# The next round's q1 and k projections put ahead of the probability transposes in a fused attention and mixture-of-experts layer

## The chip, the cores and the metric

One core of a Trainium2 chip runs the whole kernel. The metric is the device time of one execution in microseconds.

## The reference

The input x has 4 sequences of 512 tokens with 256 features. It is normalised over its features (xn). Two branches are computed from xn and multiplied:

```
xn  = layernorm(x)                                  # 2048 tokens x 256
q   = xn @ Wq   (16 heads x 128)      k, v = xn @ Wk, xn @ Wv   (4 key-value heads x 128)
q,k = rotary embedding with a per-position scale (q times it, k divided by it)
att = softmax(causal(q k^T / sqrt(128))) v          # four query heads share one key-value head
s   = att @ Wo
ffn = sum over the 2 best of 16 experts of weight * down(silu(gate) * up)  +  a shared expert
out = x + s * silu(ffn)
```

All of it is float32. The kernel keeps that precision on TensorE by splitting each operand into a float16 part ("hi") and a bfloat16 remainder ("lo") and adding three products, hi x hi, hi x lo and lo x hi (`PASSES`).

## The kernel before

Each engine has its own program, a queue worked off in the order in which it is written; semaphores tie the queues together. Nothing is planned at run time: the order on each engine is written out by hand in a function `round_` for each of them (POOL L605, ACT L781, DVE L1125, PE L1400).

Attention runs in 16 rounds, one for each pair of a sequence and a key-value head. A round has four query heads, and each head is a slot. Rounds 0 to 2 ("first", "second", "third") stand by themselves, as they also split weights and choose experts; rounds 3 to 14 are a hardware loop; round 15 is the last. While a round computes its attention, it also prepares the next round: the four query projections q0 to q3 and the key projection k of the next round are made in it, and the output projections o0 to o3 of the round before are finished in it. These share two PSUM banks, and an item waits until the item two before it has left its bank (`misc_free`).

What one head passes through, engine by engine:

- `score` (PE, L1341): q k^T of four query tiles in three units, one bank each, 12 matmuls. It waits for the lo halves of q and, in a round's first slot, of k (`rot_lo`, from POOL).
- `row_max` (DVE, L1057): mask and row maximum of each query tile, in the order of the units.
- `exponentials` (ACT, L733): exp and row sum of each tile.
- `invert_sums` (DVE, L1063): reciprocal of the four sums. It is called inside the rotation of a projection, behind that rotation's first product (L1039).
- `divide` (POOL, L533): the probabilities times those reciprocals. It releases `normed`.
- `transpose_probs` (PE, L1354): ten 128x128 transposes in three units over two banks. Units 0 and 1 (eight transposes) and unit 2 (two) are called apart. Unit 0 waits for `normed`; each unit waits for the bank that it shares with the second unit before it (`pt_lo`).
- `probs_hi` (ACT, L741) casts each unit out of PSUM, and `probs_lo` (DVE, L1069) subtracts that to get the remainder.
- `weigh_values` (PE, L1370), and `output_hi` (ACT, L756) and `output_lo` (DVE, L1075), which empty its bank.
- `project_out` (PE, L1386) and `add_projection` (DVE, L1082).

A projected q or k passes through `project` (PE, L1310, six matmuls of 512 columns), three products of the rotation (DVE, L1039, L1043, L1044), their sum (`rotate_sum`, POOL, L520), the cast to hi (`rotate_hi`, ACT, L721) and the subtraction for lo (`rotate_lo`, POOL, L527). In rounds 3 to 14 POOL also scatters the rows of one token tile to the experts, with two indirect DMAs (L550) behind slot 1's work; in round 1 and round 2 it computes the routing instead.

The order in slots 1 and 2 of a middle round, as each engine's `round_` has it (j is the slot, so head j is transposed while head j + 1 is scored):

- PE: score of head j + 1; transposes of units 0 and 1 of head j; projection (q1 in slot 1, k in slot 2); output projection j - 1; transposes of unit 2; weighing of head j - 1.
- ACT: output_hi of head 0 (slot 2 only); casts of units 0 and 1 of head j; exponentials of head j + 1; rotate_hi of q(j - 1); cast of unit 2.
- DVE: output_lo of head 0 (slot 2 only); row maxima of head j + 1; subtractions of units 0 and 1; the rotation of q1 or k, with the reciprocal of head j + 1 behind its first product; add_projection; subtraction of unit 2.
- POOL: sum of q(j - 1); divide of head j + 1; in slot 2 the sum of k; lo of q(j - 1); in slot 1 the scatter. Behind slot 2 come the lo of k, the sum of q2, the divide of the next round's head 0, and the lo of q2.

In slot 0 PE has score, projection q0, transposes of units 0 and 1, weighing of the round before's last head, values, transposes of unit 2; ACT and DVE there do the exponentials and the rotation ahead of the casts and subtractions. After slot 2 PE has projection q2, output projection o2, transposes of head 3 (units 0 and 1), weighing of head 2, the score of the next round's head 0, projection q3, transposes of unit 2, output projection o3.

Of the kernel before, what the change touches and what calls it, by code (L numbers as in the profile page):

```python
# [186 lines left out]
def build(nc, x, wq, wk, wv, wo, gate_t, w_gate_up, w_down, shared_gu, shared_down, rope, ident, mask, iota, tri, rows, digits, out):  # L187
    with ExitStack() as ctx:
# [1064 lines left out]
        def _(pe):  # L1253

            def transpose_xn(b, c, ps):
                for q in range(QT):
                    ins = pe.transpose(ps[:, q * P:(q + 1) * P], xn_t[:, b * QT + q, c * P:(c + 1) * P], ident_f[:])
                return ins

            def transpose_x_items(rd, items):  # L1260
                for name in items:
                    b, c = int(name[1]), int(name[2])
                    pe.wait_ge(xn_ready, b)
                    pe.wait_ge(misc_free, rd.item(name) - 2)
                    transpose_xn(b, c, misc_bank[rd.bank(name)]).then_inc(misc_ps, 1)
# [23 lines left out]
            def rank(rd):  # L1289
                pe.wait_ge(chosen, 1)  # L1290
                pe.wait_ge(zeroed, 2)
                pe.wait_ge(misc_free, rd.item("rank") - 2)
                ps, n = misc_bank[rd.bank("rank")], NT * E_ROUTED
                pe.matmul(ps[:, 0:n], tri_b[:], sel_b[:], start=True, stop=True)
                pe.matmul(ps[:, n:2 * n], ones_b[:], sel_b[:], start=True, stop=True).then_inc(misc_ps, 1)


            def project(rd, name):
                i, item, ps = rd.i + 1, rd.item(name), misc_bank[rd.bank(name)]
                b, g = i // NKV, i % NKV  # L1300
                if not (rd.prologue and item <= 2):
                    pe.wait_ge(misc_free, item - 2)
                tokens = [t[:, bass.ds(b * S, TOK + S)] for t in xnT]
                if name == "k":
                    chunk, w = NKV * DH, [t[:, bass.ds(g * DH, NKV * DH + DH)] for t in wkv_s]
                else:
                    chunk, w = GH * DH, [t[:, bass.ds(g * (KC * GH * DH) + int(name[1]) * DH, GH * DH + DH)] for t in wq_s]
                for c in range(KC):
                    for n, (a, m) in enumerate(PASSES):
                        ins = pe.matmul(ps[:], w[a][:, c * chunk:c * chunk + DH], tokens[m][:, c * TOK:c * TOK + S],  # L1310
                                        start=(c == 0 and n == 0), stop=(c == KC - 1 and n == 2))
                ins.then_inc(misc_ps, 1)


            def project_values(rd):
                i, item, ps = rd.i, rd.item("v"), misc_bank[rd.bank("v")]
                b, g = i // NKV, i % NKV
                pe.wait_ge(misc_free, item - 2)
                chunk = NKV * DH
                tokens = [t[:, bass.ds(b * S, TOK + S)] for t in xnT]  # L1320
                w = [t[:, bass.ds(KC * chunk + g * DH, chunk + DH)] for t in wkv_s]
                for q in range(QT):
                    for c in range(KC):
                        for n, (a, m) in enumerate(PASSES):
                            ins = pe.matmul(ps[:, q * DH:(q + 1) * DH], tokens[a][:, c * TOK + q * P:c * TOK + (q + 1) * P],
                                            w[m][:, c * chunk:c * chunk + DH],
                                            start=(c == 0 and n == 0), stop=(c == KC - 1 and n == 2))
                ins.then_inc(misc_ps, 1)


            def score(h, j, queries, keys, reuse):
                pe.wait_ge(rot_lo, queries)
                if keys is not None:
                    pe.wait_ge(rot_lo, keys)
                for u, unit in enumerate(SCORE_UNITS):
                    if reuse:
                        pe.wait_ge(exped, h * 3 + u - 2)
                    for qt, col in unit:
                        n_k = (qt + 1) * P
                        for n, (a, m) in enumerate(PASSES):  # L1340
                            ins = pe.matmul(score_bank[u][:, col:col + n_k], qT[a][:, j * S + qt * P:j * S + (qt + 1) * P], kT[m][:, 0:n_k],  # L1341
                                            start=(n == 0), stop=(n == 2))
                    ins.then_inc(scores, 1)


            def transpose_probs(h, j, units, first):
                for u in units:
                    if u == 0:
                        pe.wait_ge(normed, h + 1)
                    if not first or j > 0 or u == 2:  # L1350
                        pe.wait_ge(pt_lo, h * 3 + u - 1)
                    for kt, col in PT_UNITS[u]:
                        for qt in range(kt, QT):
                            ins = pe.transpose(pt_bank[(3 * j + u) % 2][:, col + (qt - kt) * P:col + (qt - kt + 1) * P],  # L1354
                                               probs[j % 2][:, P_AT[qt] + kt * P:P_AT[qt] + (kt + 1) * P], ident_f[:])
                    ins.then_inc(pt_ps, 1)


            def weigh_values(rd, j):
                h = rd.head(j)  # L1360
                if j == 0:
                    pe.wait_ge(misc_free, rd.item("v"))
                if j > 0 or not rd.first:
                    pe.wait_ge(o_lo, h)
                for kt in (0, 1, 3, 2):
                    n_q = (QT - kt) * P
                    if kt != 3:
                        pe.wait_ge(pt_lo, h * 3 + kt + 1)
                    for n, (a, m) in enumerate(PASSES):
                        ins = pe.matmul(o_bank[:, kt * P:S], v_s[a][:, kt * DH:(kt + 1) * DH], pT[j % 2][m][:, PT_AT[kt]:PT_AT[kt] + n_q],  # L1370
                                        start=(kt == 0 and n == 0), stop=(kt == 2 and n == 2))
                ins.then_inc(pv, 1)
# [27 lines left out]
            def round_(rd):  # L1400
                queries = [rd.i * 5 + n for n in (1, PROLOGUE.rot("q1") if rd.first else 2, 4, 5)]
                for j in range(GH - 1):
                    h = rd.head(j)
                    score(h + 1, j + 1, queries[j + 1], None, True)
                    if j == 0:
                        if rd.first:
                            pe.wait_ge(w_lo, W_FIRST)
                        if not rd.last:
                            project(rd, "q0")
                        transpose_probs(h, j, (0, 1), rd.first)  # L1410
                        if not rd.first:
                            weigh_values(rd, -1)
                        project_values(rd)
                        transpose_probs(h, j, (2,), rd.first)
                    else:
                        transpose_probs(h, j, (0, 1), rd.first)
                        if rd.first:
                            transpose_x_items(rd, X_BEFORE[j])
                        if not rd.last:
                            project(rd, ("q0", "q1", "k")[j])  # L1420
                        if not rd.first:
                            project_out(rd, j - 1)
                        transpose_probs(h, j, (2,), rd.first)
                        weigh_values(rd, j - 1)
                        if rd.second and j == 2:
                            rank(rd)
                    if rd.first:
                        transpose_x_items(rd, X_AFTER[j])
                if not rd.last:
                    project(rd, "q2")  # L1430
                if rd.first:
                    transpose_x_items(rd, X_AFTER[GH - 1])
                else:
                    project_out(rd, 2)
                transpose_probs(rd.head(3), 3, (0, 1), rd.first)
                weigh_values(rd, 2)
                if not rd.last:
                    score(rd.head(GH), 0, rd.rot("q0"), rd.rot("k"), True)
                    project(rd, "q3")
                transpose_probs(rd.head(3), 3, (2,), rd.first)  # L1440
                if rd.first:
                    router(rd)
                else:
                    project_out(rd, 3)
# [140 lines left out]
```

## Time and profile before

| | |
|---|---|
| median of 3 runs | 753.03 us (750.61 to 756.46) |
| the profiled execution | 749.65 us, span 747.8 us, granted clock 0.98 of full speed |
| PE busy | 663.3 us (89%) |
| DVE, POOL, ACT busy | 616.8 (82%), 521.7 (70%), 457.1 us (61%) |
| first and last probability transposes (L1354) start at | 35.9 and 555.2 us of the span |

Attention is therefore about the first 560 us; the experts and the end take the rest. A row of the trace gives the start in microseconds from the beginning of the span, the time it lasted, the engine, the line of the kernel, the operation, what it writes and reads, how many instructions are merged into the row, and in square brackets how long the engine had been idle before it and what ended that.

### The profile page before, as it was taken

The numbers are of one execution on the slowest core, as the hardware profiler recorded it, in microseconds if no ns is written. First come the engines' busy times: TensorE is split into PE (matmuls) and PEld (weight loads), VectorE is DVE, ScalarE is ACT, GpSimd is POOL, SyncE is SP. The second block draws the span as 40 slices with busy tenths as digits, with TensorE's granted clock in tenths as the row PEclk, the third lists the DMA queues.
The fourth block names the chain that finished last, engine by engine and source line by source line (L and its number), as shares of the span: only waits on it lengthen the run. The fifth ranks groups of instructions, "written<-read, shape, count | busy, mean of one in ns | idle before, by whom it ended". The sixth has DMA issues, their size and how long they took to land.

```text
span 747.8 us, 17742 instructions
## 1 busy us (share of the span) xinstructions
PE 663.3 (89%) x5026; PEld 470.4 (63%) x5091; DVE 616.8 (82%) x1737; ACT 457.1 (61%) x1269; POOL 521.7 (70%) x565
## 2 busy tenths in 40 slices
PE   3578879799999999999999999999986789999982
PEld 1256546566766767676676666667664468778761
DVE  7988789789999999899998999989866975445477
ACT  3685636565766657667575675656765756666542
POOL 4677768888888688886888867888654734444474
PEclk9999989999999999999999999999998999999997
DMA  9490000500000000000000000000014754444562
GB/s 308 155 317 26 1 0 2 145 16 15 14 0 14 0 14 14 0 14 0 14 7 7 14 0 14 0 14 14 1 42 147 225 89 128 132 129 133 192 254 84
DMA packets 45747, 50.40 MB, mean 67 GB/s; under 512 B 9906, under 2 KB 39058, under 8 KB 45714
## 3 DMA queue, kind: packets, MB, share of 16 engines
q1 hardware_dynamic: 41602, 39.44, 17.6%
q0 software_dynamic: 3840, 10.52, 4.0%
q8 instruction: 18, 0.29, 0.2%
q14 instruction: 15, 0.12, 0.1%
q10 hardware_dynamic: 272, 0.02, 0.0%
HBM read 31.01 MB, written 18.96 MB: 67 GB/s over the span
## 4 chain that ended last, share of the span: by engine, by line
POOL 40%; issue 19%; PE 16%; DVE 14%; ACT 5%; DMA 4%; POOLq 0%; SPq 0%; DVEq 0%; ACTq 0%
POOL arena L533 16%; POOL arena L520 9%; POOL arena L527 9%; PE bank L1497 6%; PE bank L1537 5%; POOL xs_dram L550 4%; DVE arena L381 2%; ACT arena L733 2%; PE bank L1506 2%; DMA arena<-x 1%; PE bank L1517 1%; DVE arena L1044 1%; DVE arena L1043 1%; DVE s_sb L1216 1%; DVE arena L1069 1%
## 5 line engine op out<-in xcount | busy, mean ns | idle before, releaser
L533 POOL TENSOR_TENSOR arena<-arena,rinv 128x128 f32<-128x128 f32 (+3 forms) x256 | 176.5, 721 | 104.9 <-DVE rinv L1063 104.9
L733 ACT ACTIVATE arena<-bank,nmax 128x512 f32<-128x512 f32 (+3 forms) x256 | 132.5, 534 | 63.8 <-DVE nmax L1057 63.8
L1057 DVE CUSTOM_DVE_ANT_0 bank<-bank,mask_b 128x512 f32<-128x512 f32 (+3 forms) x256 | 118.0, 517 | 13.9 <-issue 13.9
L1341 PE MATMUL bank<-arena 128*128 128x128 f16 (+6 forms) x735 | 113.5, 296 | 9.3 <-POOL arena L527 7.2
L1310 PE MATMUL bank<-xnT_hi,arena 128*128 (+1 forms) x320 | 110.4, 387 | 9.8 <-DVE arena L1044 4.9
L741 ACT CAST arena<-bank 128x512 f16<-128x512 f32 (+1 forms) x192 | 93.1, 521 | 41.7 <-PE bank L1354 40.2
L1370 PE MATMUL bank<-arena 128*128 128x512 f16 (+1 forms) x766 | 116.5, 302 | 0.2
L1069 DVE TENSOR_TENSOR arena<-bank,arena 128x512 bf16<-128x512 f32 (+1 forms) x192 | 109.0, 596 | 3.8 <-ACT arena L741 1.7
L1354 PE MATMUL bank<-ident_f,arena 128*128 128x128 f32 x640 | 92.8, 276 | 19.1 <-DVE arena L1069 12.2
L520 POOL TENSOR_TENSOR arena<-arena 128x512 f32<-128x512 f32 x77 | 98.7, 1282 | 2.5 <-DVE arena L1044 2.2
L1341 PEld LDWEIGHTS bank<-arena 128*128 128x128 f16 (+1 forms) x768 | 65.8, 98 | 49.1 <-issue 7.6
L527 POOL TENSOR_TENSOR arena<-arena 128x512 bf16<-128x512 f32 x80 | 92.5, 1161 | 4.3 <-ACT arena L721 4.3
L1386 PE MATMUL bank<-arena 128*128 (+2 forms) x768 | 94.0, 273 | 1.2 <-DVE logit L1000 0.8
L1354 PEld LDWEIGHTS bank<-ident_f,arena 128*128 128x128 f32 x640 | 73.6, 141 | 31.9 <-DVE arena L1069 16.1
L1370 PEld LDWEIGHTS bank<-arena 128*128 128x128 f16 (+1 forms) x768 | 67.6, 99 | 37.8 <-issue 1.3
L1386 PEld LDWEIGHTS bank<-arena 128*128 (+2 forms) x768 | 75.0, 98 | 19.2 <-issue 1.3
L664 POOL DMA_INDIRECT ys_dram<-arena,row_u x48 | 46.0, 959 | 58.5 <-ACT arena L875 58.5
L721 ACT CAST arena<-arena 128x512 f16<-128x512 f32 x80 | 50.3, 629 | 52.4 <-POOL arena L520 47.9
L1223 DVE TENSOR_TENSOR arena<-bank,arena 128x176 f32<-128x176 f32 x80 | 26.9, 337 | 53.8 <-ACT arena L861 52.6
L1310 PEld LDWEIGHTS bank<-xnT_hi,arena 128*128 (+1 forms) x320 | 31.8, 99 | 44.2 <-issue 8.3
L1043 DVE TENSOR_TENSOR arena<-bank,tab 64x512 f32<-64x512 f32 x80 | 55.5, 693 | 2.1
L756 ACT CAST arena<-bank 128x512 f32 (+1 forms) x64 | 38.0, 594 | 30.4 <-PE bank L1370 30.3
(150 smaller groups left out, 1251.4 us busy)
## 6 DMA issues: line engine op xcount, KB each, us to landing
xs_dram<-s_sb SPq DMA_DIRECT2D x4, 1548.0 KB, 14.3
arena<-xs_dram SPq DMA_DIRECT2D x48, 128.0 KB, 2.4
stage<-w_gate_up SPq DMA_DIRECT2D x16, 352.0 KB
arena<-ys_dram SPq DMA_DIRECT2D x8, 512.0 KB, 6.5
stage<-w_down SPq DMA_DIRECT2D x16, 176.0 KB
stage<-wq SPq DMA_DIRECT2D x4, 512.0 KB, 8.7
stage<-wo SPq DMA_DIRECT2D x4, 512.0 KB, 7.3
stage<-x SPq DMA_DIRECT2D x1, 2048.0 KB, 10.1
```

The costliest lines, as they stand in the source:

```text
L520: pool.tensor_tensor(rot_a[buf], rot_a[buf], rot_b[buf], ALU.add).then_inc(rot_add, 1)
L527: pool.tensor_tensor(dst, rot_a[buf], hi, ALU.subtract).then_inc(rot_lo, 1)
L533: ins = pool.tensor_tensor(pr, pr, rinv[:, par, qt:qt + 1].to_broadcast([P, (qt + 1) * P]), ALU.mult)
L733: ins = act.activation(probs[par][:, P_AT[qt]:P_AT[qt] + n], score_bank[u][:, col:col + n], ACT.Exp, scale=-1.0, bias=nmax[:, par, qt:qt + ...
L741: act.copy(pT[j % 2][0][:, at:at + cols], pt_bank[(3 * j + u) % 2][:, 0:cols]).then_inc(pt_hi, 1)
L1057: ins = dve.tensor_tensor_reduce(score_bank[u][:, col:col + n], score_bank[u][:, col:col + n], mask_b[:, S - n:S], -1.0, 3e38, ALU.add, AL ...
L1069: dve.tensor_tensor(pT[j % 2][1][:, at:at + cols], pt_bank[(3 * j + u) % 2][:, 0:cols], pT[j % 2][0][:, at:at + cols], ALU.subtract).then_ ...
L1310: ins = pe.matmul(ps[:], w[a][:, c * chunk:c * chunk + DH], tokens[m][:, c * TOK:c * TOK + S], start=(c == 0 and n == 0), stop=(c == KC - ...
L1341: ins = pe.matmul(score_bank[u][:, col:col + n_k], qT[a][:, j * S + qt * P:j * S + (qt + 1) * P], kT[m][:, 0:n_k], start=(n == 0), stop=(n ...
L1354: ins = pe.transpose(pt_bank[(3 * j + u) % 2][:, col + (qt - kt) * P:col + (qt - kt + 1) * P], probs[j % 2][:, P_AT[qt] + kt * P:P_AT[qt] ...
L1370: ins = pe.matmul(o_bank[:, kt * P:S], v_s[a][:, kt * DH:(kt + 1) * DH], pT[j % 2][m][:, PT_AT[kt]:PT_AT[kt] + n_q], start=(kt == 0 and n ...
L1386: ins = pe.matmul(ps[:, 0:D], heads[a][:, j * S + q * P:j * S + (q + 1) * P], w[m][:, j * D:(j + 1) * D], start=(j == 0 and n == 0), stop= ...
```

## The change

In slots 1 and 2 of every round but the first, PE's call of the transposes of units 0 and 1 moves behind the call of the projection. In the first round the order stays as it was. The last round has no projection, so its order stays as well. Only PE's program is touched.

```diff
                     else:
-                        transpose_probs(h, j, (0, 1), rd.first)
                         if rd.first:
+                            transpose_probs(h, j, (0, 1), rd.first)
                             transpose_x_items(rd, X_BEFORE[j])
                         if not rd.last:
                             project(rd, ("q0", "q1", "k")[j])
+                        if not rd.first:
+                            transpose_probs(h, j, (0, 1), rd.first)
                         if not rd.first:
                             project_out(rd, j - 1)
                         transpose_probs(h, j, (2,), rd.first)
```

## Rows read from the trace of the kernel before

**Rows 1.** The page: the chain that ended last, shares of the span by engine.

```profile
POOL 40%; issue 19%; PE 16%; DVE 14%; ACT 5%; DMA 4%; POOLq 0%; SPq 0%; DVEq 0%; ACTq 0%
```

**Rows 2.** Busy time by stretch: one loop round. Columns are named in the first line.

```profile
core 0: us, PE busy (x) PEld busy (x) DVE busy (x) ACT busy (x) POOL busy (x), PEclk, DMA share, GB/s
305.32:336.84 31.52, 30.83 (x235) 21.68 (x240) 29.04 (x85) 20.23 (x59) 24.70 (x29) 1.00 0.02 8
```

**Rows 3.** Timeline of PE in that round, to the next round's score.

```profile
305.32 1.80 PE L1341 MATMUL bank<-arena 128*128 128x512 f16 x12 [0.17 <-POOL arena L527]
...
317.00 0.44 PE L1354 MATMUL bank<-ident_f,arena 128*128 128x128 f32 x2 [0.29 <-DVE arena L1069]
...
318.90 1.04 PE L1354 MATMUL bank<-ident_f,arena 128*128 128x128 f32 x8
319.77 0.38 PE L1310 MATMUL bank<-xnT_hi,arena 128*128 x1
...
321.07 1.47 PE L1386 MATMUL bank<-arena 128*128 x12
322.38 0.38 PE L1354 MATMUL bank<-ident_f,arena 128*128 128x128 f32 x2
...
336.82 0.98 PE L1341 MATMUL bank<-arena 128*128 128x512 f16 x4 [0.15 <-POOL arena L527]
```

**Rows 4.** Timeline of DVE, same round.

```profile
306.18 0.69 DVE L1057 CUSTOM_DVE_ANT_0 bank<-bank,mask_b 128x512 f32<-128x512 f32 x1 [0.78 <-issue]
...
316.25 1.29 DVE L1069 TENSOR_TENSOR arena<-bank,arena 128x512 bf16<-128x512 f32 x2
...
320.75 1.28 DVE L1069 TENSOR_TENSOR arena<-bank,arena 128x512 bf16<-128x512 f32 x2
...
322.69 0.18 DVE L1063 RECIPROCAL rinv<-rsum 128x4 f32<-128x4 f32 x1
322.90 0.69 DVE L1043 TENSOR_TENSOR arena<-bank,tab 64x512 f32<-64x512 f32 x1
...
329.66 0.17 DVE L1063 RECIPROCAL rinv<-rsum 128x4 f32<-128x4 f32 x1
```

**Rows 5.** Timeline of ACT in slot 1 of that round.

```profile
319.54 1.07 ACT L741 CAST arena<-bank 128x512 f16<-128x512 f32 x2 [0.90 <-PE bank L1354]
320.50 0.70 ACT L733 ACTIVATE arena<-bank,nmax 128x512 f32<-128x512 f32 x1
...
322.42 0.23 ACT L733 ACTIVATION_READ_ACCUMULATOR arena<-bank,nmax 128x1 f32 x1
```

**Rows 6.** Timeline of POOL from slot 1 to the next round's score.

```profile
322.94 2.75 POOL L533 TENSOR_TENSOR arena<-arena,rinv 128x128 f32<-128x128 f32 x4 [2.97 <-DVE rinv L1063]
...
328.28 0.96 POOL L550 DMA_INDIRECT xs_dram<-compare,slot_now  x1 [0.30 <-issue]
...
330.49 2.74 POOL L533 TENSOR_TENSOR arena<-arena,rinv 128x128 f32<-128x128 f32 x4
...
334.42 2.26 POOL L527 TENSOR_TENSOR arena<-arena 128x512 bf16<-128x512 f32 x2
```

**Rows 7.** Timelines of rounds 1 (to 97), 2 (to 133) and 3.

```profile
84.24 1.05 ACT L741 CAST arena<-bank 128x512 f16<-128x512 f32 x2
96.80 0.69 ACT L733 ACTIVATE arena<-bank,nmax 128x512 f32<-128x512 f32 x1 [4.60 <-DVE nmax L1057]
...
127.87 0.18 DVE L1063 RECIPROCAL rinv<-rsum 128x4 f32<-128x4 f32 x1
129.41 2.80 POOL L533 TENSOR_TENSOR arena<-arena,rinv 128x128 f32<-128x128 f32 x4
132.26 1.09 PE L1354 MATMUL bank<-ident_f,arena 128*128 128x128 f32 x8 [1.06 <-POOL arena L533]
...
161.28 1.09 PE L1354 MATMUL bank<-ident_f,arena 128*128 128x128 f32 x8 [0.98 <-POOL arena L533]
```

**Rows 8.** Timeline of PE: the next round's first score, in rounds 3 and 14.

```profile
179.27 1.80 PE L1341 MATMUL bank<-arena 128*128 128x512 f16 x12
...
525.93 1.80 PE L1341 MATMUL bank<-arena 128*128 128x512 f16 x12 [0.17 <-POOL arena L527]
```

## The prediction

> **What bounds the kernel now.** I read the page first: the chain that ended last goes through POOL for 40% of the span and through PE for 16% [rows 1]. Then the totals of one round, from one score of a next round's first head to the next [rows 2]: 30.83 us of PE work in 31.52 us at a granted clock of 1.00, with DVE at 29.04 and POOL at 24.70. By that row alone PE is the bound and the order inside its queue is free. So I followed one round row by row. I write T01 for the eight transposes of units 0 and 1, T2 for the two of unit 2, and S for the start of the score of the next round's first head.
>
> The round closes on itself through four engines:
>
> - S (305.32) to T2 of slot 0 (317.00), 11.68 us. DVE starts the row maxima 0.86 us after S, at 306.18, and works its queue down to the subtraction at 316.25, for which T2 waits [rows 3, 4].
> - T2 of slot 0 to T01 of slot 1 (318.90), 1.90 us: T2 and the twelve matmuls of the score, back to back [rows 3].
> - T01 of slot 1 to the divide of the next head on POOL (322.94), 4.04 us. ACT sits idle 0.90 us for the transposes, casts from 319.54, only then starts the exponentials at 320.50, and has read the last sum at 322.65 [rows 5]; the reciprocal stands at 322.69 [rows 4], and POOL had been idle 2.97 us for it [rows 6].
> - That divide to the next S (336.82), 13.88 us. POOL works without a wait for another engine, its longest gap being 0.30 between its two indirect DMAs; it ends with the k subtraction at 334.42 + 2.26 = 336.68, and PE's score waits for it (0.15 and 0.17 us idle) [rows 3, 6].
>
> 11.68 + 1.90 + 4.04 + 13.88 = 31.50 us, the whole round. A cycle as long as the period has no slack: whatever is put into any piece of it lengthens every round. PE is nearly full because it is nearly as long as that cycle, and it holds one piece that counts here: the stretch ahead of T01 in slot 1.
>
> **The change, part by part.** It removes nothing and adds no instruction, DMA or wait. Slot 0 has its projection ahead already, the first round keeps its order, and the last has no projection. So 14 rounds change (1 to 14), in slots 1 and 2: score, projection, T01, output projection, T2. SP's and POOL's queues and those of ACT and DVE keep their order.
>
> *Price of the step.* The q1 projection is six weight loads and six matmuls from 319.77 to the output projection at 321.07 [rows 3], 1.30 us. Its register instructions run on PE's sequencer ahead of it; q0 already follows a score in slot 0 without trouble in the same loop, so I add nothing, and 0.2 us as an upper end. T01 itself is 0.87 us (318.90 to 319.77). That the transposes start 1.30 us later follows from the queue being in order.
>
> That price has one competitor. The Trainium skill (TensorE: Matmul & The Clock Gate, section Back-to-back issue gap) gives about 131 ns per matmul of 512 columns in a sustained stream of loads and matmuls; the six would then cost 0.79 us by that page, where the rows have 217 ns each. The rows decide.
>
> *Slot 1, rounds 4 to 14.* What waits behind T01: the casts on ACT, and behind those, on the same queue, the exponentials of the next head. The casts move from 319.54 to 320.84, the exponentials from 320.50 to 321.80, and the last sum is read at 323.95. DVE is ready earlier: it comes to its pair of subtractions (1.28 us) at 320.75 [rows 4], waits some 0.7 us for the first cast, and is through with them and with one rotation product of about 0.7 us near 323.4; so the reciprocal waits for ACT and moves from 322.69 to 323.98. POOL's divide moves by 1.29, and since nothing on POOL waits up to the k subtraction, so does S. Nothing else in this piece takes the place of the late transposes, since before the change ACT and DVE came to the reciprocal within 0.05 us of each other. Per round I take +1.30 us; the ends are 1.0 (if ACT catches up 0.3 us, about what the exponentials of the other slots gain by waiting less) and 1.5.
>
> T2 of slot 1 keeps its place: score, projection, T01 and output projection sum to the same, so it falls due at 322.38 [rows 3], and the subtraction that it needs, 0.64 us behind the first cast's end near 321.4, is done by 322.1. Cover left: some 0.2 us; without it T2 waits, on PE, which has room ahead of S (below).
>
> *Slot 2.* The same 1.30 us on the k projection moves the next reciprocal from 329.66 [rows 4] to about 330.96. POOL will reach that divide at 330.49 + 1.29 = 331.78 [rows 6], so 0.8 us of slack hide it. T2 there may wait some 0.25 us and T01 of slot 3 some 0.3 us for the divide; both lie on PE ahead of an S that now comes 1.3 us later, so they cost nothing. The wait at S takes up the rest: about 1.0 us instead of 0.16.
>
> *Rounds 1 to 3* [rows 7]. Round 1: ACT's casts in slot 1 start only at 84.24, later than the moved T01 allows, since an exponential of the router is ahead of them; in slot 2 the exponentials behind T01 wait 4.60 us for DVE, until 96.80. Nothing either way. Round 2: the reciprocal of slot 1 moves from 127.87 to 129.17, and POOL, without a pause before, reaches its divide at 129.41; in slot 2 T01 waited 1.06 us for POOL, which the projection now fills, and POOL goes on unchanged. Nothing. Round 3: T01 waited 0.98 us for POOL, until 161.28; the projection fits into that gap but for 0.16 us. So rounds 4 to 14 pay in full, eleven of them: S of round 3 stands at 179.27 and that of round 14 at 525.93 [rows 8], 31.51 us a round with no exception.
>
> *The sum.* 11 x 1.30 + 0.16 = 14.4 us. Everything after the last S follows from it (the last round, then the loads and experts behind it), so no cover there. The profiled execution took 749.65 us (span 747.8), which gives 764.1; it lies 3.4 us below the median of 753.03, from which the same sum gives 767.4. I predict 766.
>
> **The rivals.**
>
> 1. *PE is the bound and order is free.* The casts' delay is swallowed in slack that I misjudged, and the waits of T01 on POOL in rounds 2 and 3 (1.06 and 0.98 us, [rows 7]) are filled with a gain: 753.0 - 2.0 = 751, so not slower, and faster by 0.3% at the most. For it: 30.83 of 31.52 us [rows 2]. Against it: POOL's 2.97 us of idle behind the reciprocal, in every round. It decides if the reciprocal in slot 1 moves by less than 0.2 us. The Trainium skill (Trainium Kernel Development and Optimization, Best Practices) holds matmul busy time to be a bad measure for such a verdict; that chain and busy share part here bears it out. Chance 8%.
> 2. *Part of the insertion is covered.* If the six matmuls cost 0.8 us rather than 1.30 in the cycle, 11 x 0.8 = 8.8 us, 759 to 762. It would take matmuls that run closer together behind a score than they do in [rows 3], or exponentials that speed up. The 131 ns of the skill's page named above would give this too. Chance 7%.
> 3. *Both slots pay.* POOL's slack of 0.8 us in slot 2 is gone and the late k projection pushes S once more, 11 x (1.29 + 1.30 - 0.8) = 19.7 us, 769 to 773. For it: the k projection needs the bank that DVE's last q1 product frees, two products of 0.69 us [rows 4] behind the reciprocal, at about 325.6 after the change; the score ahead of that projection ends near 325.8. Chance 7%.
> 4. *The change doesn't do what it says*, as the projection is ahead in slot 0 already and waits on a free bank: excluded in slot 1, where the q0 products that free the bank are through at 316.25, when DVE turns to its subtractions [rows 4], well before 318.90.
>
> The forecast itself has 78%: 11 x 1.0 to 11 x 1.5 us on 749.65 to 753.03, that is 760.7 to 769.7. With rivals 2 and 3 the range is 758 to 772. One per cent, 7.5 us, is about what a measurement of this kernel tells from no change. Faster by more: 0.02, out of rival 1 for idle time that I have not counted. Within it: 0.10, the rest of rival 1 and the low end of rival 2. Slower: 0.88.
>
> **What would show it.** In the profile after: a round of 32.8 us from S to S; PE's wait for POOL ahead of S up from 0.16 to about 1 us; in slot 1 T01 behind the projection, ACT's casts 1.3 us later after the score, a stall on DVE ahead of its subtraction, POOL's idle time ahead of that divide near 4.3 us; rounds 1 and 2 as long as now. The prediction is wrong if the round stays at 31.5 us (rival 1), or if POOL's next divide (slot 2) waits for a reciprocal (rival 3).

## The result and the profile after

The changed kernel takes 768.73 us (median of four runs, 768.15 to 770.95), the kernel before on the same chip 752.59 us. The ratio is 1.0213, 95% interval 1.0168 to 1.0259: some 16 us slower. The profiled execution took 768.95 us with a span of 767.1 us, against 749.65 and 747.8.

The page after: two entries of the shares by line, then the costliest groups in which the idle time grew (busy and mean | idle before, and what ended it).

```profile
POOL 40%; issue 19%; PE 17%; DVE 14%; ACT 6%; DMA 3%; POOLq 0%; SPq 0%; DVEq 0%; ACTq 0%
...
L533 POOL TENSOR_TENSOR arena<-arena,rinv 128x128 f32<-128x128 f32 (+3 forms) x256 | 176.4, 720 | 121.5 <-DVE rinv L1063 121.5
...
L741 ACT CAST arena<-bank 128x512 f16<-128x512 f32 (+1 forms) x192 | 93.2, 522 | 72.8 <-PE bank L1354 71.1
L1310 PE MATMUL bank<-xnT_hi,arena 128*128 (+1 forms) x320 | 111.7, 391 | 21.8 <-DVE arena L1044 19.7
```

The chain looks as it did [rows 1]; such shares can't tell the two kernels apart. The groups can: POOL's divide waits longer for the reciprocal (121.5 us in all, 104.9 before), ACT's casts longer for the transposes (72.8, 41.7 before), and PE's projections now wait for DVE (21.8, 9.8 before).

One loop round, from S to S, with the columns of [rows 2]:

```profile
313.43:346.24 32.81, 31.15 (x239) 21.65 (x239) 29.18 (x85) 20.04 (x59) 24.69 (x29) 1.00 0.02 8
```

32.81 us instead of 31.52, with almost the same work on DVE and POOL. The rows of that round that answer to [rows 3], on PE:

```profile
313.43 1.80 PE L1341 MATMUL bank<-arena 128*128 128x512 f16 x12 [0.17 <-POOL arena L527]
...
325.11 0.44 PE L1354 MATMUL bank<-ident_f,arena 128*128 128x128 f32 x2 [0.29 <-DVE arena L1069]
...
327.01 0.38 PE L1310 MATMUL bank<-xnT_hi,arena 128*128 x1
...
328.31 1.04 PE L1354 MATMUL bank<-ident_f,arena 128*128 128x128 f32 x8
329.18 1.47 PE L1386 MATMUL bank<-arena 128*128 x12
330.49 0.38 PE L1354 MATMUL bank<-ident_f,arena 128*128 128x128 f32 x2
...
340.80 0.39 PE L1310 MATMUL bank<-xnT_hi,arena 128*128 x1 [1.22 <-DVE arena L1044]
...
346.24 1.80 PE L1341 MATMUL bank<-arena 128*128 128x512 f16 x12 [0.16 <-POOL arena L527]
```

S to T2 of slot 0 is 11.68 us, as before. The q1 projection takes 327.01 to 328.31, then T01. Two rows matter for the verdict: the wait for POOL at S is still 0.16 us, and a wait of 1.22 us for DVE stands ahead of the q2 projection at 340.80, where there was none.

DVE (answers to [rows 4]), ACT ([rows 5]) and POOL ([rows 6]) in the same round:

```profile
329.56 1.29 DVE L1069 TENSOR_TENSOR arena<-bank,arena 128x512 bf16<-128x512 f32 x2 [0.56 <-ACT arena L741]
...
332.10 0.18 DVE L1063 RECIPROCAL rinv<-rsum 128x4 f32<-128x4 f32 x1 [0.65 <-ACT arena L733]
...
339.06 0.18 DVE L1063 RECIPROCAL rinv<-rsum 128x4 f32<-128x4 f32 x1 [0.40 <-ACT arena L733]
...
339.97 0.68 DVE L1044 TENSOR_TENSOR arena<-bank,tab 64x512 f32<-64x512 f32 x1
```

```profile
328.95 1.07 ACT L741 CAST arena<-bank 128x512 f16<-128x512 f32 x2 [2.19 <-PE bank L1354]
329.90 0.71 ACT L733 ACTIVATE arena<-bank,nmax 128x512 f32<-128x512 f32 x1
```

```profile
332.35 2.75 POOL L533 TENSOR_TENSOR arena<-arena,rinv 128x128 f32<-128x128 f32 x4 [4.27 <-DVE rinv L1063]
...
339.89 2.74 POOL L533 TENSOR_TENSOR arena<-arena,rinv 128x128 f32<-128x128 f32 x4
343.83 2.27 POOL L527 TENSOR_TENSOR arena<-arena 128x512 bf16<-128x512 f32 x2
```

In slot 1 ACT is idle 2.19 us ahead of its casts (0.90 before), DVE waits for the exponentials at 332.10, and POOL's idle time grows from 2.97 to 4.27 us. In slot 2 the reciprocal (339.06) comes 0.8 us ahead of POOL's divide (339.89).

**Where the 16 us lie.** I measure from T2 of slot 0 in one round to that of the next. Round 1: no change. Round 2: 36.05 to 38.10 us, +2.05. Round 3: 32.71 to 32.98, +0.27. Rounds 4 to 14, eleven of them together: 345.89 to 360.09, +14.20, or 1.29 each. That is 16.5 us from round 1 to the last T2. The spans of the profiled pair differ by 19.3 us, the medians by 16.1; of the pair's difference a further 2.2 us stand behind attention and 0.6 ahead of round 1. From the last probability transposes to the end it is 192.6 us before, 194.8 after and 192.4 to 197.1 us in the kernels below, whose code there is the same, so I do not count that part.

Round 2, after. DVE and POOL up to slot 2's divide, and PE at S, with the granted clock of its twelve matmuls (columns of [rows 2]):

```profile
129.78 0.18 DVE L1063 RECIPROCAL rinv<-rsum 128x4 f32<-128x4 f32 x1 [0.65 <-ACT arena L733]
...
132.09 0.85 DVE L1003 TENSOR_SCALAR compare<-compare 128x256 f32<-128x256 f32 x1
...
138.09 0.16 DVE L1063 RECIPROCAL rinv<-rsum 128x4 f32<-128x4 f32 x1
```

```profile
138.33 2.75 POOL L533 TENSOR_TENSOR arena<-arena,rinv 128x128 f32<-128x128 f32 x4 [1.06 <-DVE rinv L1063]
```

```profile
147.75 2.78 PE L1341 MATMUL bank<-arena 128*128 128x512 f16 x12 [2.74 <-POOL arena L527]
150.32 0.63 PE L1310 MATMUL bank<-xnT_hi,arena 128*128 128x512 f16 x1
150.75 0.63 PE L1310 MATMUL bank<-xnT_lo,arena 128*128 128x512 bf16 x1
```

```profile
147.75:150.32 2.57, 2.57 (x12) 1.52 (x13) 1.13 (x5) 0.78 (x2) 1.13 (x1) 0.62 0.17 51
```

The same places before:

```profile
130.75 0.57 DVE L1003 TENSOR_SCALAR compare<-compare 128x256 f32<-128x256 f32 x1
...
136.33 0.17 DVE L1063 RECIPROCAL rinv<-rsum 128x4 f32<-128x4 f32 x1
```

```profile
136.61 2.75 POOL L533 TENSOR_TENSOR arena<-arena,rinv 128x128 f32<-128x128 f32 x4
```

```profile
146.02:147.64 1.62, 1.62 (x12) 1.04 (x13) 0.77 (x5) 0.00 (x0) 1.12 (x1) 1.00 0.70 177
```

```profile
146.02 1.79 PE L1341 MATMUL bank<-arena 128*128 128x512 f16 x12 [2.76 <-POOL arena L527]
```

POOL waits 1.06 us that it did not wait. The clock does the rest: the twelve matmuls take 2.57 us from start to start of what follows instead of 1.62 (146.02 to 147.64), and the two projection matmuls behind them 0.43 us each against 0.217 in the loop. The granted clock over the twelve is 0.62 against 1.00: TensorE starts them at 2.4 GHz and falls to 1.2 while they run; before it stayed at 2.4. S to the next T2 of slot 0 takes 13.15 us instead of 12.21, so of the 2.05 us some 1.1 are the wait and 0.94 the clock. The last section shows that the clock's part need not come from the change.

### The profile page after: what moved, and what is told of

Read it like the earlier page. It is cut to its first block, busy times and chain, and to the rows that moved or that the text cites. A ratio compares the mean times of both kernels' runs of the same rounds, so it can differ in the third digit from the quotient of the medians.

```text
span 767.1 us, 17806 instructions
## 1 busy us (share of the span) xinstructions
PE 669.8 (87%) x5090; PEld 470.3 (61%) x5091; DVE 619.0 (81%) x1737; ACT 455.1 (59%) x1269; POOL 521.7 (68%) x565
## 4 chain that ended last, share of the span: by engine, by line
POOL 40%; issue 19%; PE 17%; DVE 14%; ACT 6%; DMA 3%; POOLq 0%; SPq 0%; DVEq 0%; ACTq 0%
POOL arena L533 16%; POOL arena L520 9%; POOL arena L527 9%; PE bank L1499 6%; PE bank L1539 5%; POOL xs_dram L550 4%; ACT arena L733 2%; DVE arena L381 2%; PE bank L1508 2%; PE bank L1519 1%; DVE s_sb L1216 1%; DVE arena L1044 1%; DVE arena L1043 1%; ACT arena L741 1%; DVE s_sb L1213 1%
## 5 line engine op out<-in xcount | busy, mean ns | idle before, releaser
L533 POOL TENSOR_TENSOR arena<-arena,rinv 128x128 f32<-128x128 f32 (+3 forms) x256 | 176.4, 720 | 121.5 <-DVE rinv L1063 121.5
L741 ACT CAST arena<-bank 128x512 f16<-128x512 f32 (+1 forms) x192 | 93.2, 522 | 72.8 <-PE bank L1354 71.1
L1310 PE MATMUL bank<-xnT_hi,arena 128*128 (+1 forms) x320 | 111.7, 391 | 21.8 <-DVE arena L1044 19.7
L1057 DVE CUSTOM_DVE_ANT_0 bank<-bank,mask_b 128x512 f32<-128x512 f32 (+3 forms) x256 | 118.1, 516 | 14.3 <-issue 14.3
L1341 PE MATMUL bank<-arena 128*128 128x512 f16 (+7 forms) x768 | 115.9, 301 | 7.2 <-POOL arena L527 6.9
L1370 PE MATMUL bank<-arena 128*128 128x512 f16 (+7 forms) x768 | 116.6, 302 | 0.1
L1354 PE MATMUL bank<-ident_f,arena 128*128 128x128 f32 x640 | 93.1, 276 | 20.3 <-DVE arena L1069 14.4
L527 POOL TENSOR_TENSOR arena<-arena 128x512 bf16<-128x512 f32 x80 | 92.5, 1161 | 5.5 <-ACT arena L721 5.5
L1310 PE MATMUL bank<-xnT_lo,arena 128*128 (+1 forms) x160 | 62.6, 391 | 0.0
L1039 DVE TENSOR_TENSOR arena<-bank,tab 128x512 f32<-128x512 f32 x80 | 54.8, 684 | 3.2 <-PE bank L1310 3.0
```

The costliest lines, as they stand in the source:

```text
L527: pool.tensor_tensor(dst, rot_a[buf], hi, ALU.subtract).then_inc(rot_lo, 1)
L533: ins = pool.tensor_tensor(pr, pr, rinv[:, par, qt:qt + 1].to_broadcast([P, (qt + 1) * P]), ALU.mult)
L741: act.copy(pT[j % 2][0][:, at:at + cols], pt_bank[(3 * j + u) % 2][:, 0:cols]).then_inc(pt_hi, 1)
L1057: ins = dve.tensor_tensor_reduce(score_bank[u][:, col:col + n], score_bank[u][:, col:col + n], mask_b[:, S - n:S], -1.0, 3e38, ALU.add, AL ...
```

## Experiments

The theory is that of the prediction: in slots 1 and 2 ACT's casts stand ahead of the exponentials of the next head, so what is put ahead of the transposes on PE delays the reciprocal, and with it POOL. Twelve kernels were run. "Period" is T2 of slot 0 to T2 of slot 0 in the middle of the loop, 31.52 us before and 32.81 after. Ratios are to the kernel before on the same chip.

**Slot 1 alone** (`e1_slot1`) and **slot 2 alone** (`e2_slot2`, with `j == 2`). Against the changed kernel:

```diff
-                        if rd.first:
+                        late = not rd.first and j == 1
+                        if not late:
                             transpose_probs(h, j, (0, 1), rd.first)
+                        if rd.first:
                             transpose_x_items(rd, X_BEFORE[j])
                         if not rd.last:
                             project(rd, ("q0", "q1", "k")[j])
-                        if not rd.first:
+                        if late:
                             transpose_probs(h, j, (0, 1), rd.first)
```

> Only slot 1 has its projection (q1) ahead of the transposes; slot 2 keeps the order of before. Theory (the delay of slot 1's transposes goes through ACT's casts and exponentials into POOL's divide, and slot 2 has slack): the whole loss stays, a round of 32.8 us from score to score, some 767 us. Rival A (the new wait of PE ahead of the q2 projection, 1.21 us for DVE's k products in every round of the changed kernel, is the cost, and it comes from slot 2): that wait shrinks, the round goes back to 31.5 us, some 753 us. Rival B (each slot pays half): 32.2 us a round, some 760 us.

771.66 us, ratio 1.0212 [1.0174, 1.0249], period 32.82. The move in slot 1 alone costs all of it. PE in the loop:

```profile
304.13 1.09 PE L1354 MATMUL bank<-ident_f,arena 128*128 128x128 f32 x8 [1.04 <-POOL arena L533]
...
315.20 1.80 PE L1341 MATMUL bank<-arena 128*128 128x512 f16 x12 [0.21 <-POOL arena L527]
```

The new wait on PE now stands ahead of T01 of slot 2, for POOL's divide, and again not at S.

> Only slot 2 has its projection (k) ahead of the transposes; slot 1 as before. Theory: slot 2's slack is the 0.66 us by which POOL came to its divide after the reciprocal was ready; alone, the 1.30 us use it up and the rest pays: 0.65 us a round, 32.2 us from score to score, 11 x 0.65 = 7 us, some 760 us, with POOL now waiting about 0.7 us for the reciprocal in slot 2. The two slots then don't add up: both together cost 1.29, not 1.94. Rival A (slot 2's new wait ahead of q2 is the cost): 1.3 us a round, some 767 us. If slot 2 had ample slack: 753 us.

766.67 us, ratio 1.0138 [1.0104, 1.0171], period 32.48: slot 2 alone costs 0.96 us, not 0.65. POOL behaves as expected, with 0.65 us of wait; PE loses more:

```profile
306.45 2.75 POOL L533 TENSOR_TENSOR arena<-arena,rinv 128x128 f32<-128x128 f32 x4 [0.65 <-DVE rinv L1063]
```

```profile
307.94 0.39 PE L1310 MATMUL bank<-xnT_hi,arena 128*128 x1 [1.34 <-DVE arena L1044]
```

The q2 projection needs the bank that DVE's last k product empties. That product stands behind the reciprocal, and so behind the late exponentials. 1.30 us late there, less what PE had to spare ahead of S, is 0.98. In the kernel before that spare time was 0.32 us: from the start of the weighing below, its twelve matmuls take 1.63 us, to 336.50, and S stands at 336.82 [rows 3].

```profile
334.87 1.79 PE L1370 MATMUL bank<-arena 128*128 128x512 f16 x12
```

The costs of the two slots do not add up (1.30 + 0.96 against 1.29 together): they run side by side.

**POOL's stretch shortened.** The scatter's two indirect DMAs go behind the sum of q2, off the stretch from slot 1's divide to the k subtraction; with the change (`e3_after_scatter_late`) and with slot 1 alone (`e4_slot1_scatter_late`):

```diff
-                    if j == 1 and rd.tile() is not None:
-                        scatter()
                 if not rd.last:
                     rotate_lo("k", rd.rot("k"))
                     rotate_sum("q2", rd.item("q2"))
+                if rd.tile() is not None:
+                    scatter()
+                if not rd.last:
                     divide(rd.head(GH), 0)
```

> The changed kernel, with POOL's two indirect DMAs of the token rows moved from behind slot 1 to behind the sum of q2, where POOL is idle for about 3 us. That takes 2.44 us out of POOL's stretch from slot 1's divide to the k subtraction. Theory (a cycle through PE, ACT, DVE and POOL): slot 1's path falls to 30.4 us and slot 2's takes over, as its reciprocal is 1.3 us late and POOL now waits for it: 32.2 us a round, half of the loss back, some 760 us. Rival (the loss sits on PE and DVE, with POOL's work off the path): 32.8 us a round, 767 us.

768.81 us, ratio 1.0159 [1.0108, 1.0209], period 32.48, where 32.2 had been expected. POOL no longer makes PE wait at S. The wait of 1.22 us at q2 is left, and the period is that of slot 2 alone.

> Projection ahead in slot 1 alone, and the indirect DMAs late. Theory: slot 1's path is 30.4 us, slot 2's reciprocal hardly late, so PE and DVE bound the round at about 31.35 us: the loss of 14 us is gone altogether although the transposes of slot 1 are as late as in the changed kernel; some 751 to 754 us. Rival (late transposes cost by themselves, on PE, ACT or DVE): 32.8 us a round, 767 us.

765.27 us, ratio 1.0122 [1.0088, 1.0156], period 32.44: a miss by over 1 us. POOL no longer ends the round, yet only 0.37 us of the 1.29 came back. PE in the loop:

```profile
303.08 1.09 PE L1355 MATMUL bank<-ident_f,arena 128*128 128x128 f32 x8 [1.03 <-POOL arena L533]
...
313.78 1.79 PE L1342 MATMUL bank<-arena 128*128 128x512 f16 x12
```

S has no wait now, but T01 of slot 2 still waits for the divide: 1.03 us there in place of 0.17 at S, which is 0.86 of the 0.92 us that are left. In the kernel before, T01 of slot 1 to the end of that divide is 318.90 to 322.94 + 2.75 = 325.69 [rows 3, 6], 6.8 us; PE's own work between the two T01 was 6.96 us, the second standing at 325.86. So a second way round had 0.2 us of slack at most, and with the one through POOL's whole stretch shortened, this one holds nearly as much.

**Half of the projection ahead** (`e5_half`): `project` is split; in slot 1 three of the q1 matmuls stand ahead of T01, three behind it, slot 2 as before.

```diff
+                        half = not rd.first and not rd.last and j == 1
+                        if half:
+                            project(rd, "q1", 0)
+                        transpose_probs(h, j, (0, 1), rd.first)
...
-                            project(rd, ("q0", "q1", "k")[j])
-                        if not rd.first:
-                            transpose_probs(h, j, (0, 1), rd.first)
+                            project(rd, ("q0", "q1", "k")[j], 1 if half else None)
```

> Half the dose: in slot 1 only, three of q1's six matmuls stand ahead of the transposes and three behind; slot 2 as before. Theory (a closed cycle without slack, so time in is time out): 0.65 us more a round, 32.15 to 32.2 us from score to score, 11 x 0.65 + some 1 us in round 2 = 8 us over the kernel before. Rival (the cost comes with the swap itself, from a wait or from register instructions, not from the time inserted): 32.8 us a round, or none.

759.65 us, ratio 1.0093 [1.0066, 1.012], period 32.16. Half of the matmuls cost half: three cost 0.64 us a round and six 1.30 (e1), 0.21 to 0.22 us for each, which is what one of them takes. Neither size shows a first part that was free.

**The exponentials made independent of the transposes** (`e6_exp_first`): in slots 1 and 2 ACT does the exponentials ahead of the casts, DVE the rotation and reciprocal ahead of the subtractions, and PE puts T2 behind the weighing. `e7_exp_first_old_order` is the same with the projection behind the transposes, `e8_exp_first_scatter_late` is e6 with the late scatter.

```diff
-                        probs_hi(rd.head(j), j, (0, 1))
+                        if rd.first:
+                            probs_hi(rd.head(j), j, (0, 1))
                         exponentials(h, par)
+                        if not rd.first:
+                            probs_hi(rd.head(j), j, (0, 1))
...
-                        probs_lo(rd.head(j), j, (0, 1))
                         if rd.first:
+                            probs_lo(rd.head(j), j, (0, 1))
                             x_items_lo(rd, X_BEFORE[j])
                         rope(("q0", "q1", "k")[j], (h, par))
                         if not rd.first:
+                            probs_lo(rd.head(j), j, (0, 1))
...
-                        transpose_probs(h, j, (2,), rd.first)
+                        if rd.first:
+                            transpose_probs(h, j, (2,), rd.first)
                         weigh_values(rd, j - 1)
+                        if not rd.first:
+                            transpose_probs(h, j, (2,), rd.first)
```

> The changed PE order of projections and transposes, but in slots 1 and 2 ACT does the exponentials ahead of the casts, DVE the rotation with its reciprocal ahead of the subtractions, and PE the last two transposes behind the weighing. The late transposes then stand in front of nobody's exponentials. Theory (all of the loss goes through ACT's queue: casts, exponentials, reciprocal; then on to POOL's divide and to the bank that q2 waits for): no loss is left, 31.2 to 31.6 us a round, within 1% of the kernel before, perhaps 1 to 4 us faster. Rival (late transposes cost on PE or DVE by themselves): 32 us and more, 6 to 14 us slower than the kernel before.

764.65 us, ratio 1.0153 [1.0096, 1.021], period 32.21, where 31.2 to 31.6 had been expected: a miss, at the rival's figure. The next run shows that the rival's reason is not it either.

> The same order on ACT, DVE and for the last two transposes as in the run before it, with the projection behind the transposes as in the kernel before. It tells what that reordering is worth by itself. Theory: with the exponentials independent of the transposes, the place of the projection is free, so this run and the one before it agree within 3 us. Rival (projection first is harmful of itself): this one is 10 us or more ahead of it.

761.9 us, ratio 1.0119 [1.006, 1.0179], period 32.20. The two differ by 0.01 us a round. With the order on ACT, on DVE and of T2 changed, the place of the projection costs nothing; in the original order it costs 1.29. These kernels change the three together, so they don't tell which of them it takes, and e11 below shows what the equality rests on. The rearrangement itself costs 0.69 us. DVE and PE in e6:

```profile
294.70 0.18 DVE L1066 RECIPROCAL rinv<-rsum 128x4 f32<-128x4 f32 x1 [0.62 <-ACT arena L733]
...
296.33 1.29 DVE L1072 TENSOR_TENSOR arena<-bank,arena 128x512 bf16<-128x512 f32 x2
```

```profile
297.08 0.44 PE L1358 MATMUL bank<-ident_f,arena 128*128 128x128 f32 x2 [0.26 <-DVE arena L1072]
```

The reciprocal waits 0.62 us for the exponentials and holds up two rotation products and the subtractions behind it, for which T2 then waits.

> Projection first, exponentials first, and POOL's two indirect DMAs moved to behind the sum of q2. Theory: POOL's path and the bank path are both short now, and what is left is PE itself with the piece that DVE bounds ahead of slot 0's last transposes: 31.0 to 31.4 us a round, 2 to 6 us faster than the kernel before. If POOL still bounded the round, this would gain 2.4 us a round over the run without it.

762.36 us, ratio 1.0118 [1.0065, 1.0171], period 32.19, a miss again: POOL is off the path in that arrangement.

**The reciprocal taken out of DVE's way.** It moves behind the second rotation product, in the kernel before for slot 0 alone (`e9_before_recip_slot0`), in e6 for slots 0 to 2 (`e10_exp_first_recip_late`); here the first:

```diff
-                if inverted_head is not None:
+                if inverted_head is not None and not name == "q0":
                     invert_sums(*inverted_head)
                 dve.tensor_tensor(rot_b[buf][0:half, :], ps[half:DH, :], tab[half:DH, sin, :], ALU.mult)
+                if inverted_head is not None and name == "q0":
+                    invert_sums(*inverted_head)
```

> The kernel before, with DVE's reciprocal of slot 0 one rotation product later (behind the second instead of the first). DVE sits idle 0.52 us there for ACT's exponentials in every round; the second product would fill that. It lies in the stretch from the next round's score to slot 0's last transposes, which is part of every cycle found so far. Theory: about 0.4 us less a round (PE, at 30.83 us, comes next), 31.1 us from score to score, 4 to 6 us faster than the kernel before. Rival (POOL's divide, now 0.2 us later, or PE takes it back): no change.

750.11 us against 754.37, ratio 0.995 [0.9923, 0.9976], period 31.04. The wait of T2 of slot 0 for DVE [rows 3] is gone, worth 0.48 us a round, as expected.

> Projection first and exponentials first as in the sixth run, and the reciprocal one rotation product later in slots 0, 1 and 2, which fills DVE's idle 0.5 to 0.6 us in each. Theory: the 0.69 us a round that the reordering cost is DVE's idle time ahead of the last transposes of slots 1 and 2, so it goes away, and slot 0's with it: 31.0 to 31.3 us a round, 2 to 6 us faster than the kernel before although the projection is ahead in every slot. Rival (the reordering costs for another reason): it stays at 32 us, some 9 us slower.

742.56 us against 754.37, ratio 0.9854 [0.9827, 0.9881]: faster than both kernels, with the projection ahead in every slot, and by more than the 2 to 6 us expected. One round (columns of [rows 2]), and DVE and PE in slot 1:

```profile
305.48:336.10 30.62, 30.41 (x235) 21.79 (x238) 29.11 (x85) 20.32 (x60) 24.69 (x28) 1.00 0.02 9
```

```profile
317.48 0.68 DVE L1042 TENSOR_TENSOR arena<-bank,tab 128x512 f32<-128x512 f32 x1
...
319.80 1.29 DVE L1074 TENSOR_TENSOR arena<-bank,arena 128x512 bf16<-128x512 f32 x2
```

```profile
320.74 0.38 PE L1360 MATMUL bank<-ident_f,arena 128*128 128x128 f32 x2
```

No row of PE in that round shows a wait; at least 30.41 of 30.62 us are work (this record lacks some matmuls: it has 235, that of e11 240).

**The order put back in that kernel** (`e11_exp_first_recip_late_old_order`: e10 with the projection behind the transposes).

> The kernel before with the exponentials ahead of the casts and the reciprocal behind the second rotation product, the projection behind the transposes as in the kernel before: e10 with the order of the projection put back. Theory (with the exponentials independent of the transposes and the reciprocal no longer holding the subtractions up, TensorE alone sets the round; it has 30.41 us of work in e10's period of 30.63, and the place of the projection is free): 30.6 to 30.7 us a round, 741 to 744 us, the ratio to e10's within 0.3%. Rival (the projection's place still costs, TensorE being full only because something else moves with it): a period other than e10's by 0.3 us or more, 3 us or more either way.

752.15 us against 753.11, ratio 0.9999 [0.9975, 1.0023], period 31.44. The theory's "free" is refuted: here the changed order is worth 0.81 us a round, and e10 and e11, the same kernel but for the edit of this document, stand at 0.9854 and 0.9999 of the kernel before. One round of e11, and DVE and PE in slot 1:

```profile
313.40:344.85 31.45, 30.91 (x240) 21.70 (x238) 29.41 (x85) 20.39 (x60) 24.70 (x28) 1.00 0.02 8
```

```profile
326.02 0.69 DVE L1042 TENSOR_TENSOR arena<-bank,tab 128x512 f32<-128x512 f32 x1 [0.48 <-PE bank L1316]
...
328.35 1.29 DVE L1074 TENSOR_TENSOR arena<-bank,arena 128x512 bf16<-128x512 f32 x2
```

```profile
329.10 0.44 PE L1360 MATMUL bank<-ident_f,arena 128*128 128x128 f32 x2 [0.27 <-DVE arena L1074]
```

DVE now takes the rotation first, so it waits 0.48 us for the projection where e10's DVE did not wait (317.48); the subtractions, and T2 behind them, come later: in slot 1 T2 stands 7.40 us behind T2 of slot 0 instead of 6.97, and slot 2, where DVE waits another 0.19 us for the projection, adds 0.39 to these 0.43. In e7 DVE waited 0.47 us for the projection too, but the reciprocal's wait for the exponentials (0.62 us in e6) swallowed it, which is why e6 and e7 were equal.

**The changed kernel with the late reciprocal alone** (`e12_after_recip_late`: the edit of e9, for slots 0, 1 and 2).

> The changed kernel with one edit: the reciprocal of slots 0, 1 and 2 behind the second rotation product instead of ahead of it; casts ahead of exponentials as in the kernel before. Theory (of the 1.29 us a round that the change costs, the casts held up by the projection are the cause and stay; the reciprocal's place is worth in slot 0 what it was worth in the kernel before, 0.48 us a round from 31.52 to 31.04): 32.3 to 32.5 us a round, 762 to 765 us. Rival (the loss comes from the late reciprocal holding VectorE's queue, the rotation products behind it and so the q2 projection's bank): the wait of 1.2 us ahead of the q2 projection goes and the period falls to 31.0 to 31.6 us, 749 to 755 us.

763.74 us, ratio 1.0147 [1.0124, 1.017], period 32.37: 0.44 less than the changed kernel, close to e9's 0.48, and the rest of the loss stays. PE in the loop:

```profile
306.85 0.39 PE L1312 MATMUL bank<-xnT_hi,arena 128*128 x1 [0.70 <-DVE arena L1046]
312.96 1.80 PE L1343 MATMUL bank<-arena 128*128 128x512 f16 x12 [0.82 <-POOL arena L527]
```

The wait at q2 shrinks from 1.22 to 0.70 us, and the one at S grows from 0.16 to 0.82: POOL's arrival sets S, and PE merely waits in one place or the other.

## Why the prediction was right, and where it was not

**Slot 1, right in mechanism and size.** Six matmuls from 327.01 to 328.31 are the 1.30 us of the step; the casts, the exponentials, the reciprocal and POOL's divide follow by that much, with POOL's idle time at 4.27 us (4.3 predicted) and a period longer by 1.29. e1 shows that slot 1 suffices, e5 that the cost goes with the matmuls, and e12 that the late reciprocal's place in DVE's queue is not the cause. e6 and e7 fit, as the cost is gone where the exponentials and the rotation no longer stand behind the transposes, but they change three orders at once.

**Rounds, right but for round 2.** Round 1 pays nothing, round 3 0.27 us (0.16 predicted), rounds 4 to 14 pay in full, 14.2 us of the 14.3 worked out for them. The step that failed is the one on round 2, "POOL goes on unchanged. Nothing." It compared slot 1's late reciprocal with POOL alone (129.17 against 129.41). It did not ask what stands behind that reciprocal in DVE's own queue: the routing operations (L1003 to L1005) and the row maxima of the next slot. So slot 2's reciprocal came at 138.09 instead of 136.33, 1.1 us later in a round that began 0.6 us later, and POOL, which had not waited there, waits 1.06 us. Some 0.7 of the 1.1 us came through the queue; the other 0.4 arose on the way, as L1003 and L1005 took 0.85 and 0.58 us instead of 0.57 and 0.45. A wait of POOL's divide in slot 2 was one of the prediction's own signs of being wrong; it shows in round 2, not in the loop. The other 0.94 us of that round is the clock in the profiled execution, of which no row of before gave a sign. With these 2.05 us the sum is 16.5 instead of the 14.46 that the prediction rounds to 14.4, against 16.1 between the medians. How near 766 lies to 768.73 is partly luck: it was chosen between two starting times 3.4 us apart.

**Slot 2, right in the outcome, wrong in the reason.** It adds nothing on top of slot 1, and POOL's 0.8 us of slack is there as predicted. But "The wait at S takes up the rest: about 1.0 us instead of 0.16" was wrong: that time appears ahead of the q2 projection, 1.22 us for DVE's last k product. I had left that product out of slot 2's consequences, although its reciprocal is inserted right ahead of it. e2 shows what that hides: alone, slot 2 costs 0.96 us.

**"A cycle as long as the period has no slack" is right; but this cycle is not the only one that counts.** e3 and e4 shorten its POOL part, and get 0.33 and 0.37 us back out of 1.29, since two others are within a few tenths of it: T01 of slot 1 through the divide to T01 of slot 2, and slot 2's transposes through DVE's k products to the q2 projection.

**The rivals.** Rival 1 (order is free) fell in this kernel. Its bound does exist: in e10 PE is the bound, at 30.41 of 30.62 us, and even so the old order is not free (e11). Rival 2 (part covered) fell: e1 and e5 give 0.21 to 0.22 us for each of the matmuls, and the exponentials of slot 1, first start to last sum read, take 2.16 us against 2.15 before. The 131 ns for a matmul of 512 columns that the Trainium skill gives (TensorE: Matmul & The Clock Gate, section Back-to-back issue gap) is not seen here; in the loop these matmuls start 217 ns apart in every kernel of this study. Rival 3 (both slots pay) fell as a sum in the loop, though the wait that it looked for on the k projection's bank turned up one projection later, on q2's. Rival 4 is excluded as predicted: the moved projection starts at 327.01 without a wait.

## What to carry to other kernels

Before moving work inside one engine's queue, write down for both pieces which engine takes each of them, and what stands behind that consumer in its own queue; in this kernel, what the others took first was best put first. The same edit cost 1.29 us a round where ACT and DVE took the transposes first, nothing where a wait covered both orders, and gained 0.81 us where DVE took the projection first. When a closed chain explains the whole period, look for the second and third longest before promising anything from shortening it.

## What was not expected of the hardware

After almost the same idle time on PE ahead of S in round 2, TensorE kept 2.4 GHz in some kernels (2.74 to 2.77 us in the kernel before, e2, e3 and e5) and fell to 1.2 GHz in others while the twelve matmuls ran (2.70 to 2.86 us in the changed kernel, e1, e4, e9, e10 and e11). It also stayed up in e6 to e8, with 2.3 us, and fell in e12, with 3.44. Idle time further back does not tell them apart either: the changed kernel and e3 have the same waits ahead of it, T2 of slot 2 and the q2 projection, and the same at S. PE in e3:

```profile
139.43 0.44 PE L1355 MATMUL bank<-ident_f,arena 128*128 128x128 f32 x2 [1.73 <-DVE arena L1070]
142.13 0.39 PE L1311 MATMUL bank<-xnT_hi,arena 128*128 128x512 f16 x1 [0.63 <-DVE arena L1045]
150.15 1.79 PE L1342 MATMUL bank<-arena 128*128 128x512 f16 x12 [2.74 <-POOL arena L527]
```

The changed kernel has 1.73 and 0.63 us there as well, and its twelve matmuls at S take 2.78 us. Its round 2 is 38.10 us long, that of e3 37.18, the 0.94 us of the clock. What decides is open. It can't be the order of this document alone: e9 keeps the old order and has the same waits ahead of S as the kernel before, to 0.03 us, yet its clock fell, and its twelve matmuls took 3.05 us instead of 1.62. Each kernel has one trace, so whether a kernel's clock falls there every time is not shown.

In the same round DVE's L1003 took 0.85 or 0.86 us in the changed kernel, e1, e3 and e4, and 0.47 to 0.57 in all the others, on the same operands. In those four POOL went over from the divide (L533) to the next subtraction (L527) while L1003 ran; in the others POOL was in the divide throughout. So what POOL does at that moment goes with the difference; no run here shows how.
